# Postnorm decoder layer in fp32: Q and the output projection directly behind V3, the next step's scores ahead of the values

## The chip, the cores and the metric

The kernel runs on one core of a Trainium2 chip. The metric is device time in microseconds of one execution, from inputs in HBM to the output in HBM, as the median of several runs. One execution each was profiled.

## The reference

A decoder layer on x of 4 x 512 x 512 in three parts, each followed by a residual add and a LayerNorm. The change is in the first, a gated slot attention with 16 heads:

```
q, k, v, s, g = x@Wq, x@Wk, x@Wv, clip(x@Ws, -32, 32), x@Wg   # heads of 64, 64, 128, 64, 128
z = cumlogsumexp(s, time); gdec = exp(z[t-1] - z[t]); p = exp(s - z)
hk[t] = hk[t-1]*gdec + k[t] p[t]^T        ; ok[t] = (q[t]/8) hk[t]
pv = softmax(ok)
hv[t] = hv[t-1]*gdec + p[t] v[t]^T        ; o[t] = pv[t] hv[t]
o = o * rsqrt(mean(o^2) + eps) * g_norm_weight * silu(g)
x = layernorm(x + o @ Wo)
```

Then come a cross attention with 32 query heads over ctx_512 and a ternary feed-forward network with 1408 inner units.

## The kernel before

The attention runs as 32 steps n = 0 to 31, each for one pair of heads (n // 4) and one batch element (n % 4) of 512 rows. The recurrences are computed in 8 chunks of 64 rows: products inside a chunk (with a causal mask) plus products with the running state of the chunks before.

Wide products are done as three fp32r matmuls of high and low halves (`mm3`, L61 to L63), in groups of 12 matmuls of 128x512. The projections of step n+1 are woven into step n on TensorE: S, K, V0 to V3 (`VG` to `VG + 3`; values and gate together, one row tile of 128 each) and Q. They alternate between two PSUM banks, so each waits until ScalarE and VectorE have read the group before the last.

Every engine works through its own list in the order of the code; only semaphores hold it. TensorE's list in a step n is: `key_scores` (L1226, products of queries and keys of one chunk), `key_states` (L1243), projections S and K, `slots` (L1295), `states` (L1267), `slots_from_states` (L1307), V0, V1, V2, `transpose_weights` (the slot weights pv, L1153), V3, `diagonals` (L1253), `values_from_states` (L1321), Q, `project_out` (o of the step before times Wo, four row tiles of 6 matmuls), `values` (L1332). `project_out` writes its tiles in turn to two banks, `okb` and `tb`; its tiles 2 and 3 wait until VectorE has added tiles 0 and 1 to acc (`added`). `key_states` of the next step uses the same two banks and waits for all four adds. `key_scores` and `diagonals` both write the two banks `ch`, which VectorE reads with the causal mask (`mask_scores` L1953, `mask_diagonal_blocks` L1971) into the tile `causal`.

The rows of the keys (keys with time on the partitions) are made by VectorE and by DMA: VectorE transposes blocks of 32 (`turn_keys`, into the memory of `causal`), SyncE writes them to HBM (`put_keys`) and reads them back (`get_keys`), and ScalarE copies them (`rows_of_keys`, L1697). The exponentials e, their running sum z and the gated output of the step before go the same way, in the order e, output, z, keys on SyncE's queue. ScalarE's list in the later half of a step is: `high_turned` (high half of the turned output), `rows_of_keys`, the copy and tanh of V3 (L1669, L1671), the copy of Q (L1650), sums of squares. VectorE's is: `low_turned` (L2014), the first half of `inverse_z` (L1939), `mask_diagonal_blocks`, the gating of V3 (L1915), the second half of `inverse_z`, four `add_out` (L2022), `gated_output` (L2076), and then, of the next step, `mask_scores`, the other half of `gated_output`, running key states, clip, `turn_e`, running z and the rest. `mask_diagonal_blocks` also waits for `rows_of_keys`, since the transposed keys lie in `causal`.

The change applies to the steps n <= `LATE_OUT` = 28. From 29 on the order is another, with the output projection ahead of the diagonals.

Of the kernel before, what the change touches and what calls it, by code (L numbers as in the profile page):

```python
# [11 lines left out]
P = 128  # L12
B = 4
# [3 lines left out]
TT = T // P  # L17
# [11 lines left out]
PROJ = 7  # L29
S, K, VG, Q = 0, 1, 2, 6  # L30
# [112 lines left out]
def layer_program(nc, x, ctx_in, Wq, Wk, Wv, Wg, Ws, Wo, gw, gate_w, up_w, down_w, gate_s, up_s, down_s, out,  # L143
# [6 lines left out]
    with ExitStack() as ctx:  # L150
# [10 lines left out]
        def sem(name):  # L161
            return ctx.enter_context(nc.semaphore("a_" + name))
# [14 lines left out]
        keys = sb("keys", [P, T])  # L177
# [3 lines left out]
        eT = sb("eT", [P, 2, T])  # L181
# [11 lines left out]
        running = flat[:, 0:T]  # L193
# [25 lines left out]
        tb = ps[:, 4, :]  # L219
# [36 lines left out]
        proj_done = sem("proj_done")  # L256
        scores_done = sem("scores_done")
        key_states_done = sem("key_states_done")
        keysT_done = sem("keysT_done")
        diag_done = sem("diag_done")  # L260
        states_done = sem("states_done")
        oT_done = sem("oT_done")
# [2 lines left out]
        okT_done = sem("okT_done")  # L265
        pvT_done = sem("pvT_done")
        o_done = sem("o_done")
        e_done = sem("e_done")

        queries_kept = sem("queries_kept")  # L270
        keys_kept = sem("keys_kept")
# [11 lines left out]
        z_turned = sem("z_turned")  # L283
        z_out = sem("z_out")
        z_back = sem("z_back")
        zT_done = sem("zT_done")
        weights_ready = sem("weights_ready")
        eT_ready = sem("eT_ready")
        v_ready = sem("v_ready")
# [783 lines left out]
        def _(pe):  # L1073
# [73 lines left out]
            def max_pair(u, i):  # L1147
                for par in range(2):
                    max_scores(u, u, i, par)

            def transpose4(bank, blocks):
                for i, src in enumerate(blocks):
                    last = pe.transpose(bank[:, i * P:(i + 1) * P], src, ident[:, :])  # L1153
                return last
# [62 lines left out]
            def key_scores(n):  # L1217

                pe.wait_ge(keys_kept, n + 1)
                pe.wait_ge(queries_kept, n + 1)  # L1220
                wait(pe, diag_masked, n)
                for c in range(CHUNKS):
                    i, r = c // 2, c % 2
                    rows = slice(c * CHUNK, (c + 1) * CHUNK)
                    for h in range(2):
                        mm = pe.matmul(ch[h][HALF[r], i * CHUNK:(i + 1) * CHUNK], keys[HALF[h], rows],  # L1226
                                       queries[HALF[h], rows], start=True, stop=True)
                mm.then_inc(scores_done, 1)
# [18 lines left out]
            def diagonals(n):  # L1247

                for c in range(CHUNKS):
                    i, r = c // 2, c % 2  # L1250
                    rows = slice(c * CHUNK, (c + 1) * CHUNK)
                    for h in range(2):
                        mm = pe.matmul(ch[h][HALF[r], i * CHUNK:(i + 1) * CHUNK], eT[HALF[h], n % 2, rows],  # L1253
                                       wT[HALF[h], (c ^ h) * CHUNK:((c ^ h) + 1) * CHUNK], start=True, stop=True)
                mm.then_inc(diag_done, 1)
# [56 lines left out]
            def values_from_states(n):  # L1312

                ob = value_banks(n)
                pe.wait_ge(state_ready, (CHUNKS - 1) * (n + 1))
                if LATE_OUT < n < NSTEP - 1:
                    pe.wait_ge(added, 4 * n)
                for c in range(1, CHUNKS):
                    i, r = c // 2, c % 2
                    for h in range(2):  # L1320
                        pe.matmul(ob[h][HALF[r ^ h], i * P:(i + 1) * P],  # L1321
                                  wT[HALF[h], (c ^ h) * CHUNK:((c ^ h) + 1) * CHUNK],
                                  state[HALF[h], c - 1, :], start=(c == 1 or c == 2), stop=False, skip_group_check=True)

            def values(n, j):

# [9 lines left out]

            def transpose_e(m):
                pe.wait_ge(eT_ready, m + 1)
                transpose4(tb, [eT[:, m % 2, i * P:(i + 1) * P] for i in range(TT)]).then_inc(e_done, 1)

            def transpose_keys(m):
                pe.wait_ge(keys_kept, m + 1)
                wait(pe, wT_ready, m)
                transpose4(okb, [keys[:, i * P:(i + 1) * P] for i in range(TT)]).then_inc(keysT_done, 1)

            def transpose_z():
                pe.wait_ge(scan_done, 1)
                transpose4(ob[0], [running[:, i * P:(i + 1) * P] for i in range(TT)]).then_inc(zT_done, 1)

            def transpose_weights(n):  # L1350
                pe.wait_ge(weights_ready, n + 1)
# [3 lines left out]
            def step(n, p, j, first):  # L1355
                b1, pair1 = (j + 1) % B, p if j < B - 1 else p + 1

                def next_project(*groups):
                    for i in groups:
                        project(n + 1, i, b1, pair1)  # L1360

                into = n == NSTEP - 2
                key_scores(n)
                key_states(n)
                next_project(S, K)
                slots(n)
                states(n, j)
                slots_from_states(n)
                next_project(VG, VG + 1)
                pair0 = p if j else p - 1  # L1370
                if at(n, 0):
                    pe.wait_ge(state_ready, CHUNKS - 1)
                    transpose_x(2, range(KT))
                if at(n, 1):
                    pe.wait_ge(okn_ready, n + 1)
                    transpose_x(3, (0, 1))
                if into:
                    pe.wait_ge(okn_ready, n + 1)
                    transpose_operands(0, 0, 0)
                    transpose_operands(0, 0, 1)  # L1380
                next_project(VG + 2)
                transpose_weights(n)
                if at(n, 1):
                    transpose_x(3, (2, 3))
                if into:
                    pe.wait_ge(opsT_ready, 1)
                    transpose_operands(0, 0, 2)
                    pe.wait_ge(opsT_ready, 2)
                    transpose_operands(0, 0, 3)
                next_project(VG + 3)  # L1390
                if into:
                    pe.wait_ge(opsT_ready, 3)
                    transpose_operands(0, 0, 4)
                    pe.wait_ge(wT_ready, n + 1)
                    max_pair(0, 0)
                if n > LATE_OUT:
                    project_out(n, pair0, (0, 1))
                    if into:
                        max_pair(0, 1)
                    project_out(n, pair0, (2, 3))  # L1400
                pe.wait_ge(wT_ready, n + 1)
                if at(n, 0) or at(n, 1):
                    pe.wait_ge(xlo_ready, (n + 3) * KT)
                if into:
                    pe.wait_ge(opsT_ready, TILES)
                    max_pair(0, 2)
                diagonals(n)
                values_from_states(n)
                if into:
                    max_pair(0, 3)  # L1410
                next_project(Q)
                if not first and n <= LATE_OUT:
                    project_out(n, pair0, (0, 1, 2, 3))
                if into:
                    max_pair(0, 4)
                pe.wait_ge(proj_done, PROJ * (n + 2))
                values(n, j)

            def last_step(n):
# [195 lines left out]
        def _(act):  # L1615
# [34 lines left out]
                nc.scalar.copy(queries[:, :], src).then_inc(queries_kept, 1)  # L1650

            def copy_key_rows(m):
                act.wait_ge(keysT_done, m + 1)
                nc.scalar.copy(key_rows[:, :, :].rearrange("p i c -> p (i c)"), okb)\
                    .then_inc(key_rows_ready, 1)

# [47 lines left out]
                nc.scalar.copy(wT, tb).then_inc(wT_ready, 1)  # L1704

            def copy_e(m):
                act.wait_ge(e_done, m + 1)
                nc.scalar.copy(e[:, :, :].rearrange("p i c -> p (i c)"), tb).then_inc(e_ready, 1)

            def square_sums(n, half):  # L1710
# [156 lines left out]
        def _(dve):  # L1867
# [72 lines left out]

            def first_inverse_z():

                dve.wait_ge(zT_done, 1)
                z = ob[0].rearrange("p (i h m) -> p i h m", i=TT, h=2)
                rows = rz[:, :].rearrange("p (i h m) -> p i h m", i=TT, h=2)
                nc.vector.reciprocal(rows[:, :, 0], z[:, :, 0])
                for r in range(2):
                    nc.vector.reciprocal(rows[HALF[r], :, 1], z[HALF[1 - r], :, 1]).then_inc(rz_ready, 1)
# [69 lines left out]
            def add_out(n, b, tiles):  # L2018
                for t in tiles:
                    wait(dve, wo_done, 4 * (n - 1) + t + 1)  # L2020
                    a = acc[:, TT * b + t, :]
                    nc.vector.tensor_tensor(a, a, out_banks(n)[t % 2], ALU.add).then_inc(added, 1)  # L2022
# [58 lines left out]
            def step(n, p, j, first):  # L2081
# [32 lines left out]
                    low_turned(n)  # L2114
                if late:
                    inverse_z(n + 1, (0,))
                    mask_diagonal_blocks(n)
                gating(n + 1, VG + 3, b1)
                if into:
                    reduce_max(0, 0, 0)  # L2120
# [16 lines left out]
                    norm.apply(dve, j - 1, j - 1, j - 1)  # L2137
                inverse_z(n + 1, (1,) if late else (0, 1))
                if not first and late:
                    add_out(n, (j - 1) % B, (0, 1, 2, 3))  # L2140
                gated_output(n, j, 0)

            def last_step(n):
# [244 lines left out]
```

## Time and profile before

| | us |
|---|---|
| median of 3 runs | 1826.91 (1825.39 to 1828.23) |
| the profiled execution, its time | 1825.38 |
| its span in the trace | 1823.7 |
| TensorE (PE) busy | 1781.5 (98%) |
| VectorE (DVE) busy | 1421.3 (78%) |
| ScalarE (ACT) busy | 754.8 (41%) |
| GpSimd (POOL) busy | 594.2 (33%) |

Busy times are sums over the span; TensorE's matmuls are pipelined, so a record of 0.39 us starts every 0.23 us. A wait is the idle time ahead of an instruction, put down to what released it last. The attention loop takes some 1040 us of the span, the rest is cross attention and feed-forward. PEld is TensorE's loading of weights, SPq SyncE's queue of DMAs. An fp32 matmul of the code stands as two in the records, so 16 matmuls are x32.

### The profile page before, as it was taken

To read this page: it belongs to the slowest core of one execution; us is meant where nothing else is said; L and a number is where in the kernel's file an instruction comes from. 1 tells how busy PE (TensorE), PEld (TensorE's weight loads), DVE (VectorE), ACT (ScalarE), POOL (GpSimd) and SP (SyncE) were. 2 spreads that over 40 slices of the span, in tenths; PEclk is the share of its full clock that TensorE was granted. 3 is DMA by queue.
4 is the path that set the end of the run, shared out by engine and by line. 5 is a ranking of instruction groups with operands and counts; after the bars stand their busy time and mean duration, and the time that the engine had idled before them with its cause. 6 is when DMAs were issued, how large, how long until landed. Compare 5 with 4: busy or idle time off the path is not lost.

```text
span 1823.7 us, 39286 instructions
## 1 busy us (share of the span) xinstructions
PE 1781.5 (98%) x15604; PEld 1303.6 (71%) x15604; DVE 1421.3 (78%) x2555; ACT 754.8 (41%) x1885; POOL 594.2 (33%) x595
## 2 busy tenths in 40 slices
PE   9999999999999999999998799999999999999998
PEld 7788888888887888888886644443434488888886
DVE  5778887878888788888787889999999665555556
ACT  3433333333333333333333248888888622122223
POOL 3042250443332513514432332344423233232332
PEclk9999999999999999999999889999999999999999
DMA  4425334442434252434333001111111111111102
GB/s 149 125 64 145 82 97 113 104 123 77 117 101 126 62 150 77 111 100 120 85 89 96 3 20 29 28 28 29 29 29 20 25 22 29 20 28 25 21 15 92
DMA packets 218550, 127.91 MB, mean 70 GB/s; under 512 B 100096, under 2 KB 198144, under 8 KB 218368
## 3 DMA queue, kind: packets, MB, share of 16 engines
q1 hardware_dynamic: 218368, 125.40, 27.0%
q8 instruction: 124, 2.03, 0.5%
q14 instruction: 58, 0.48, 0.1%
HBM read 72.90 MB, written 44.30 MB: 64 GB/s over the span
## 4 chain that ended last, share of the span: by engine, by line
PE 87%; DVE 5%; ACT 3%; SPq 2%; DMA 2%; issue 1%; POOL 0%; POOLq 0%; DVEq 0%; ACTq 0%
PE a_ps L61 20%; PE a_ps L62 19%; PE a_ps L63 19%; PE a_ps L1137 6%; PE a_ps L1099 5%; PE a_ps L1121 3%; PE a_ps L1081 2%; ACT x_prob L1809 2%; PE a_ps L1332 2%; PE a_ps L1153 2%; PE a_ps L1321 1%; PE a_ps L1267 1%; PE a_ps L1253 1%; PE a_ps L1144 1%; PE a_ps L1295 1%
## 5 line engine op out<-in xcount | busy, mean ns | idle before, releaser
L1873 DVE TENSOR_REDUCE a_raw_qks<-a_ps 128x1 f32<-128x512 f32 x512 | 321.2, 683 | 19.8 <-PE a_ps L1099 19.0
L1809 ACT ACTIVATE x_prob<-a_ps 128x512 f32<-128x512 f32 x512 | 280.0, 609 | 63.4 <-PE a_ps L1121 61.8
L61 PE MATMUL a_ps<-a_vg_hi,a_xT_lo 128*128 128x512 f32 x512 | 207.0, 404 | 0.3 <-DVE a_eT L1910 0.3
L63 PE MATMUL a_ps<-a_vg_hi,a_xT_hi 128*128 128x512 f32 x512 | 200.6, 392 | 0.0
L62 PE MATMUL a_ps<-a_vg_lo,a_xT_hi 128*128 128x512 f32 x512 | 200.1, 391 | 0.0
L917 POOL TENSOR_TENSOR a_f<-a_rs 128x8 f32<-128x8 f32 x32 | 6.4, 199 | 584.6 <-ACT a_flat L1719 584.6
L61 PE MATMUL a_ps<-a_xT_hi,a_qks_lo 128*128 128x512 f32 x384 | 157.2, 409 | 0.4 <-DVE a_xT_lo L1904 0.4
L62 PE MATMUL a_ps<-a_xT_lo,a_qks_hi 128*128 128x512 f32 x384 | 150.7, 392 | 0.0
L63 PE MATMUL a_ps<-a_xT_hi,a_qks_hi 128*128 128x512 f32 x384 | 149.6, 390 | 0.0
L1099 PE MATMUL a_ps<-a_xT_lo,a_xT_hi 64*128 64x512 f32 x384 | 143.8, 462 | 5.1 <-DMA a_xT_lo<-a_xT_lo 2.5
L1719 ACT ACTIVATE a_flat<-a_ps 128x128 bf16<-128x128 f32 x256 | 67.3, 278 | 181.8 <-PE a_ps L1332 174.4
L1121 PE MATMUL a_ps<-a_xT_hi,a_xT_lo 64*128 64x512 f32 x384 | 140.9, 452 | 0.6 <-ACT x_prob L1809 0.5
L2022 DVE TENSOR_TENSOR acc<-acc,a_ps 128x512 f32<-128x512 f32 x128 | 87.2, 683 | 68.9 <-PE a_ps L63 68.5
L61 PE MATMUL a_ps<-a_xT_hi,f_gu_lo 128*128 128x512 f32 x352 | 137.4, 390 | 1.0 <-POOL f_gu_lo L1016 1.0
L1137 PE MATMUL a_ps<-x_prob,x_values 128*32 128x512 f32 x1024 | 137.0, 608 | 0.0
L63 PE MATMUL a_ps<-a_xT_hi,f_gu_hi 128*128 128x512 f32 x352 | 137.0, 389 | 0.0
L62 PE MATMUL a_ps<-f_xT_lo,f_gu_hi 128*128 128x512 f32 x352 | 137.0, 389 | 0.0
L1099 PEld LDWEIGHTS a_ps<-a_xT_lo,a_xT_hi 64*128 64x128 f32 x384 | 61.0, 188 | 101.0 <-issue 42.6
L1669 ACT COPY a_v<-a_ps 128x256 f32<-128x256 f32 x128 | 47.5, 371 | 206.2 <-PE a_ps L63 206.2
L2259 DVE TENSOR_TENSOR acc<-acc,a_ps 128x512 f32<-128x512 f32 x172 | 113.9, 685 | 0.0
L63 PEld LDWEIGHTS a_ps<-a_vg_hi,a_xT_hi 128*128 128x128 f32 x512 | 96.4, 188 | 21.2
L61 PEld LDWEIGHTS a_ps<-a_vg_hi,a_xT_lo 128*128 128x128 f32 x512 | 96.4, 188 | 20.8 <-DVE a_eT L1910 0.4
(205 smaller groups left out, 4107.3 us busy)
## 6 DMA issues: line engine op xcount, KB each, us to landing
a_og_blocks<-a_og_turn SPq DMA_DIRECT2D x120, 128.0 KB, 2.4
a_og_turn<-a_og_blocks SPq DMA_DIRECT2D x30, 512.0 KB, 4.4
a_e_blocks<-a_e_turn SPq DMA_DIRECT2D x124, 64.0 KB, 1.8
a_e_turn<-a_e_blocks SPq DMA_DIRECT2D x31, 256.0 KB, 3.2
a_z_blocks<-a_og SPq DMA_DIRECT2D x124, 64.0 KB, 2.5
a_key_blocks<-a_causal SPq DMA_DIRECT2D x124, 64.0 KB, 3.4
a_causal<-a_key_blocks SPq DMA_DIRECT2D x31, 256.0 KB, 2.8
a_raw_vg<-in_L_attn_Wv_dram SPq DMA_DIRECT2D x8, 512.0 KB, 5.6
```

The lines of the kernel that those rows point to most:

```text
L61: pe.matmul(out, w_lo, x_hi, start=start, stop=False)
L62: pe.matmul(out, w_hi, x_lo, start=False, stop=False)
L63: return pe.matmul(out, w_hi, x_hi, start=False, stop=stop)
L1099: pe.matmul(max_bank(u, q, i, par), qs[q][HALF[par], tile, st * P:(st + 1) * P], ks[q][(tile // 2) ^ par][HALF[par], :], start=True, stop= ...
L1121: pe.matmul(score_bank(q, s, par), ks[q][g ^ par][HALF[par], t * P:(t + 1) * P], qs[q][HALF[par], 2 * g + pair, :], start=True, stop=True) ...
L1137: mm = pe.matmul(avb[32 * i:32 * (i + 1), :], cv[:, q, t, g, :], prob[i % 2][:, (s + i // 2) % 4, :], start=(t == 0), stop=(t == TT - 1))
L1669: nc.scalar.copy(v[:, b % 2, i - VG, :], bank[:, 0:2 * DV]).then_inc(v_ready, 1)
L1719: sq = nc.scalar.activation(squares[:, g, 0:DV], ob[half][:, t * P:(t + 1) * P], ACT.Square, scale=DV ** -0.5, accum_out=crossed_sums[:, t ...
L1809: nc.scalar.activation(prob[par][:, s % 4, :], score_bank(q, s, par), ACT.Exp, scale=X_SCALE).then_inc(exp_done[par], 1)
L1873: nc.vector.tensor_reduce(nm[:, q % 2, i % 4, par, i // 4:i // 4 + 1], max_bank(u, q, i, par), AX.X, ALU.max, negate=True).then_inc(max_re ...
L2022: nc.vector.tensor_tensor(a, a, out_banks(n)[t % 2], ALU.add).then_inc(added, 1)
L2259: nc.vector.tensor_tensor(a, a, down_bank(t), ALU.add).then_inc(f_added, 1)
```

## The change

For n <= 28, TensorE's order behind V3 becomes: Q, `project_out`, `diagonals`, `values_from_states`, `key_scores` of step n+1, `values`, and then `key_states` of step n+1. The wait of `values` for the projections is replaced by one for `values_from_states` (`values_begun`). On VectorE `mask_diagonal_blocks` goes from ahead of V3's gating to between the third and the fourth `add_out`. Three semaphores used once or per prologue are merged into one, `first_turned`.

```diff
@@ values_from_states
-                        pe.matmul(ob[h][HALF[r ^ h], i * P:(i + 1) * P],
+                        mm = pe.matmul(ob[h][HALF[r ^ h], i * P:(i + 1) * P],
...
+                if n <= LATE_OUT:
+                    mm.then_inc(values_begun, 1)
@@ step of TensorE
-                key_scores(n)
+                if first or n > LATE_OUT + 1:
+                    key_scores(n)
                 key_states(n)
...
-                pe.wait_ge(wT_ready, n + 1)
...
+                if n <= LATE_OUT:
+                    next_project(Q)
+                    if not first:
+                        project_out(n, pair0, (0, 1, 2, 3))
+                pe.wait_ge(wT_ready, n + 1)
                 diagonals(n)
                 values_from_states(n)
...
-                next_project(Q)
-                if not first and n <= LATE_OUT:
-                    project_out(n, pair0, (0, 1, 2, 3))
+                if n > LATE_OUT:
+                    next_project(Q)
...
-                pe.wait_ge(proj_done, PROJ * (n + 2))
+                if n <= LATE_OUT:
+                    key_scores(n + 1)
+                    pe.wait_ge(values_begun, n + 1)
+                else:
+                    pe.wait_ge(proj_done, PROJ * (n + 2))
                 values(n, j)
@@ step of VectorE
                 if late:
                     inverse_z(n + 1, (0,))
-                    mask_diagonal_blocks(n)
                 gating(n + 1, VG + 3, b1)
...
                 inverse_z(n + 1, (1,) if late else (0, 1))
                 if not first and late:
-                    add_out(n, (j - 1) % B, (0, 1, 2, 3))
+                    add_out(n, (j - 1) % B, (0, 1, 2))
+                if late:
+                    mask_diagonal_blocks(n)
+                if not first and late:
+                    add_out(n, (j - 1) % B, (3,))
                 gated_output(n, j, 0)
```

TensorE around the end of a step in the middle of the loop, before. `a_flat` holds the slot weights, `a_wo` and `a_oT` are the operands of the output projection; `...` stands for the rest of a group.

```order
L63 MATMUL a_ps<-a_vg_hi,a_xT_hi 128x512
L1253 MATMUL a_ps<-a_flat,a_eT 64x64 [waits a_wT_ready]
L1321 MATMUL a_ps<-a_state,a_flat 64x128 [waits a_state_ready]
L61 MATMUL a_ps<-a_xT_hi,a_qks_lo 128x512 [waits a_q_ready,a_gate_ready]
...
L61 MATMUL a_ps<-a_wo_hi,a_oT_lo 128x512 [waits a_oTlo_ready,a_wo_ready]
...
L61 MATMUL a_ps<-a_wo_hi,a_oT_lo 128x512 [waits a_added]
...
L1332 MATMUL a_ps<-a_v,a_causal 64x128 [waits a_diag_masked,a_proj_done]
L1226 MATMUL a_ps<-a_queries,a_keys 64x64 [waits a_diag_masked,a_queries_kept,a_keys_kept]
L1243 MATMUL a_ps<-a_e,a_key_rows 64x64 [waits a_wT_ready,a_added,a_e_ready,a_key_rows_ready]
```

The same place after the change (its lines are shifted by one or ten).

```order
L63 MATMUL a_ps<-a_vg_hi,a_xT_hi 128x512
L61 MATMUL a_ps<-a_xT_hi,a_qks_lo 128x512 [waits a_q_ready,a_gate_ready]
...
L61 MATMUL a_ps<-a_wo_hi,a_oT_lo 128x512 [waits a_oTlo_ready,a_wo_ready]
...
L61 MATMUL a_ps<-a_wo_hi,a_oT_lo 128x512 [waits a_added]
...
L1252 MATMUL a_ps<-a_flat,a_eT 64x64 [waits a_wT_ready]
L1320 MATMUL a_ps<-a_state,a_flat 64x128 [waits a_state_ready]
L1225 MATMUL a_ps<-a_queries,a_keys 64x64 [waits a_diag_masked,a_queries_kept,a_keys_kept]
L1333 MATMUL a_ps<-a_v,a_causal 64x128 [waits a_diag_masked,a_values_begun]
L1242 MATMUL a_ps<-a_e,a_key_rows 64x64 [waits a_wT_ready,a_added,a_e_ready,a_key_rows_ready]
```

Diagonals and values from states moved behind the output projection, and the scores of the next step ahead of the values.

VectorE in the same part of the step, before: low half of the turned output, `inverse_z`, mask, V3's gating, `inverse_z`, the adds, the gated output.

```order
L2014 TENSOR_TENSOR a_oT_lo<-a_og_turn,a_oT_hi 128x4x8x32 [waits a_oThi_ready]
L1939 RECIPROCAL a_rz<-a_og 128x2x4x32 [waits a_weights_ready,a_z_back]
L1971 TENSOR_TENSOR a_causal<-a_ps,a_mask 128x256 [waits a_key_rows_ready,a_diag_done]
L1971 TENSOR_TENSOR a_causal<-a_ps,a_mask 128x256
L1915 SCALAR_TENSOR_TENSOR a_gate<-a_gate,a_ps 128x256 [waits a_tanh_ready]
L1939 RECIPROCAL a_rz<-a_og 128x2x4x32
L2022 TENSOR_TENSOR acc<-acc,a_ps 128x512 [waits a_wo_done] x4
L2076 TENSOR_TENSOR a_og<-a_ps,a_gate 128x4x128 [waits a_rz_ready,a_o_done]
```

And after:

```order
L2023 TENSOR_TENSOR a_oT_lo<-a_og_turn,a_oT_hi 128x4x8x32 [waits a_oThi_ready]
L1948 RECIPROCAL a_rz<-a_og 128x2x4x32 [waits a_weights_ready,a_z_back]
L1924 SCALAR_TENSOR_TENSOR a_gate<-a_gate,a_ps 128x256 [waits a_tanh_ready]
L1948 RECIPROCAL a_rz<-a_og 128x2x4x32
L2031 TENSOR_TENSOR acc<-acc,a_ps 128x512 [waits a_wo_done] x3
L1980 TENSOR_TENSOR a_causal<-a_ps,a_mask 128x256 [waits a_key_rows_ready,a_diag_done]
L1980 TENSOR_TENSOR a_causal<-a_ps,a_mask 128x256
L2031 TENSOR_TENSOR acc<-acc,a_ps 128x512 [waits a_wo_done]
L2085 TENSOR_TENSOR a_og<-a_ps,a_gate 128x4x128 [waits a_rz_ready,a_o_done]
```

The mask moved behind three of the four adds.

## Rows read from the trace of the kernel before

**Rows 1.** Stretches: length, busy us of each engine, granted clock, DMA share, GB/s.
```profile
99.07:940.43 841.36, 840.76 (x9505) 689.35 (x9505) 683.44 (x1242) 280.08 (x918) 284.24 (x236) 1.00 0.39 103
49.60:56.40 6.80, 5.50 (x21) 5.11 (x22) 4.34 (x11) 2.86 (x5) 0.00 (x0) 0.50 0.69 193
```

**Rows 2.** TensorE's timeline of one step: start, duration, line, operands, count.
```profile
503.87 1.10 PE L1332 MATMUL a_ps<-a_v,a_causal 64*64 64x128 f32 x32
504.80 0.64 PE L1226 MATMUL a_ps<-a_queries,a_keys 64*64 64x64 f32 x32
505.26 0.65 PE L1243 MATMUL a_ps<-a_e,a_key_rows 64*64 64x64 f32 x28
...
524.74 0.39 PE L63 MATMUL a_ps<-a_vg_hi,a_xT_hi 128*128 128x512 f32 x1
525.06 0.69 PE L1253 MATMUL a_ps<-a_flat,a_eT 64*64 64x64 f32 x32
525.57 1.05 PE L1321 MATMUL a_ps<-a_state,a_flat 64*64 64x128 f32 x28
526.55 0.50 PE L61 MATMUL a_ps<-a_xT_hi,a_qks_lo 128*128 128x512 f32 x1
...
532.17 0.39 PE L61 MATMUL a_ps<-a_wo_hi,a_oT_lo 128*128 128x512 f32 x1
...
534.98 1.10 PE L1332 MATMUL a_ps<-a_v,a_causal 64*64 64x128 f32 x32
```

**Rows 3.** ScalarE's timeline of the same step: key rows, and V3's tanh.
```profile
527.75 0.62 ACT L1697 COPY a_key_rows<-a_causal 128x512 f32<-128x512 f32 x1 [2.57 <-DMA a_causal<-a_key_blocks]
...
528.54 0.39 ACT L1671 ACTIVATE a_gate<-a_ps 128x256 f32<-128x256 f32 x1
```

**Rows 4.** VectorE's timeline of the same step.
```profile
525.22 1.23 DVE L2014 TENSOR_TENSOR a_oT_lo<-a_og_turn,a_oT_hi 128x1024 fp32r<-128x1024 f32 x1 [1.82 <-ACT a_oT_hi L1685]
...
528.48 0.76 DVE L1971 TENSOR_TENSOR a_causal<-a_ps,a_mask 128x256 f32<-128x256 f32 x2 [0.37 <-ACT a_key_rows L1697]
529.15 0.41 DVE L1915 SCALAR_TENSOR_TENSOR a_gate<-a_gate,a_ps 128x256 f32<-128x256 f32 x1
529.48 1.75 DVE L1939 RECIPROCAL a_rz<-a_og 128x256 f32<-128x256 f32 x1
531.14 0.63 DVE L2022 TENSOR_TENSOR acc<-acc,a_ps 128x512 f32<-128x512 f32 x1
```

**Rows 5.** Waits in the 27 steps: us in total, times, longest.
```profile
ACT a_key_rows L1697 <- DMA a_causal<-a_key_blocks: 72.3, 27, 3.9
```

**Rows 6.** The chain that ended last, in the slowest of the 27 steps.
```profile
535.97 0.15 PE a_ps L1332 x4
...
552.34 4.88 DMA a_key_blocks<-a_causal
...
559.97 0.63 ACT a_key_rows L1697
...
563.43 0.56 DVE acc L2022
...
564.03 0.50 PE a_ps L61
```

**Rows 7.** Timelines: `values` ahead of, and key rows in, the first and last step.
```profile
99.07 1.10 PE L1332 MATMUL a_ps<-a_v,a_causal 64*64 64x128 f32 x32
...
122.79 0.62 ACT L1697 COPY a_key_rows<-a_causal 128x512 f32<-128x512 f32 x1 [2.95 <-DMA a_causal<-a_key_blocks]
...
909.32 1.10 PE L1332 MATMUL a_ps<-a_v,a_causal 64*64 64x128 f32 x32
...
932.67 0.62 ACT L1697 COPY a_key_rows<-a_causal 128x512 f32<-128x512 f32 x1 [2.40 <-DMA a_causal<-a_key_blocks]
```

**Rows 8.** The same two timelines of the step with the least distance.
```profile
878.22 1.10 PE L1332 MATMUL a_ps<-a_v,a_causal 64*64 64x128 f32 x32
...
901.14 0.62 ACT L1697 COPY a_key_rows<-a_causal 128x512 f32<-128x512 f32 x1 [2.33 <-DMA a_causal<-a_key_blocks]
```

More of the change, by code:

```diff
@@ L258, in layer_program @@
         key_states_done = sem("key_states_done")
-        keysT_done = sem("keysT_done")
         diag_done = sem("diag_done")
@@ L267, in layer_program @@
         o_done = sem("o_done")
-        e_done = sem("e_done")
+        first_turned = sem("first_turned")
         queries_kept = sem("queries_kept")
@@ L285, in layer_program @@
         z_back = sem("z_back")
-        zT_done = sem("zT_done")
+        values_begun = sem("values_begun")
         weights_ready = sem("weights_ready")
@@ L1338, in transpose_e @@
                 pe.wait_ge(eT_ready, m + 1)
-                transpose4(tb, [eT[:, m % 2, i * P:(i + 1) * P] for i in range(TT)]).then_inc(e_done, 1)
+                transpose4(tb, [eT[:, m % 2, i * P:(i + 1) * P] for i in range(TT)]).then_inc(first_turned, 1)
             def transpose_keys(m):
@@ L1343, in transpose_keys @@
                 wait(pe, wT_ready, m)
-                transpose4(okb, [keys[:, i * P:(i + 1) * P] for i in range(TT)]).then_inc(keysT_done, 1)
+                transpose4(okb, [keys[:, i * P:(i + 1) * P] for i in range(TT)]).then_inc(first_turned, 1)
             def transpose_z():
                 pe.wait_ge(scan_done, 1)
-                transpose4(ob[0], [running[:, i * P:(i + 1) * P] for i in range(TT)]).then_inc(zT_done, 1)
+                transpose4(ob[0], [running[:, i * P:(i + 1) * P] for i in range(TT)]).then_inc(first_turned, 1)
             def transpose_weights(n):
@@ L1652, in copy_key_rows @@
             def copy_key_rows(m):
-                act.wait_ge(keysT_done, m + 1)
+                act.wait_ge(first_turned, 2)
                 nc.scalar.copy(key_rows[:, :, :].rearrange("p i c -> p (i c)"), okb)\
@@ L1706, in copy_e @@
             def copy_e(m):
-                act.wait_ge(e_done, m + 1)
+                act.wait_ge(first_turned, 1)
                 nc.scalar.copy(e[:, :, :].rearrange("p i c -> p (i c)"), tb).then_inc(e_ready, 1)
@@ L1941, in first_inverse_z @@
             def first_inverse_z():
-                dve.wait_ge(zT_done, 1)
+                dve.wait_ge(first_turned, 3)
                 z = ob[0].rearrange("p (i h m) -> p i h m", i=TT, h=2)
```

## Prediction

> **What bounds the kernel now.** I read the waits first, then TensorE's timeline of one step, then ScalarE's and VectorE's of the same step. The change touches the 29 steps n = 0 to 28 of the attention loop. Of these, 27 (n = 2 to 28) look alike: they fill 841.36 us, 31.16 us each, with TensorE busy for 840.76 of them at a granted clock of 1.00 [rows 1]. So TensorE has almost no idle time, and what could be won on it is only the cost of changing between 128x128 and 64x64 work. The second thing to see is how near a loop over the other engines comes. I count it from the end of `values` of the step before, which I call zero. In the step of rows 2 it is 503.87 + 1.10 = 504.97. From there VectorE works through gating, masks, running sums and transposes, SyncE sends the keys through HBM, and ScalarE copies the key rows at 527.75, that is K = 22.78 after zero [rows 2, 3]. Only behind that copy, in ScalarE's order, stand V3's copy and tanh, so V3's gating on VectorE comes at 529.15, the second half of `inverse_z` at 529.48, and the first `add_out` at 531.14, ending 531.77 [rows 4]. TensorE needs that add to reuse its bank for the third tile of the output projection, which starts at 532.17 [rows 2]. **The slack of this loop is 0.35 us of 31.** ScalarE waited for the keys' transfer in all 27 steps, 72.3 us in all [rows 5]. In the slowest step the slack is used up: the chain runs from `values` over the write of the keys (4.88 us) to the key rows at 559.97, the add at 563.43 (to 563.99) and TensorE's third tile at 564.03 [rows 6].
>
> How firmly is K tied to zero? In [rows 7] the first and the last of the 27 steps have K = 122.79 - 100.17 = 22.62 and 932.67 - 910.42 = 22.25; the least is 901.14 - 879.32 = 21.82 [rows 8], the largest 559.97 - 536.12 = 23.85 [rows 6]. The mean over all 27, read one by one in this way, is 22.5.
>
> **The change, part by part.**
>
> *One stretch of 64x64 work less.* Diagonals and values from states stood alone between V3 and Q; now they, the next scores, `values` and the key states are one stretch. Entering costs 525.06 - 524.74 = 0.32 against the usual pitch of 0.23, so 0.09. Leaving: the 28 records of L1321 take 526.55 - 525.57 = 0.98; at the 0.029 a record that L1332 shows (504.80 - 503.87 over 32) they would take 0.81, so 0.17, and the first wide matmul behind lasts 0.50 and not 0.39, so 0.11 more [rows 2]. Together 0.37 us a step gained on TensorE, as long as nothing waits.
>
> *A wait inside the new stretch.* `key_scores` of the next step writes the banks that `mask_diagonal_blocks` reads. Before, Q and the four output tiles (some 8 us) stood between and hid the mask at no cost. Now only values from states do. From the first diagonal: its group drains after 0.69, a semaphore takes 0.05 (from the add's end 563.99 to 564.03), the two masks 0.76, the semaphore back 0.05 [rows 4, 6]: 1.55. TensorE's own work up to there is 0.51 + 0.81 = 1.32. So 0.23 us of waiting, on the path. The lower bound is 0; the upper is 0.9, if VectorE is still in an add of 0.63 when the diagonals are done. I take 0.23: the third add begins with its tile's end, 1.9 us before the diagonals drain.
>
> *Q and the output projection earlier.* Q (12 matmuls, 2.72) starts right behind V3. V3 ends at 524.74 + 0.23, 20.0 after zero, and now 19.5, since the scores (0.46) no longer stand at the step's start. V2's gating, which frees Q's bank, lies on VectorE before an idle stretch of 1.82 that ended at 525.22 [rows 4], so 18.4 after zero: no wait. The low half of the turned output ended at 525.22 + 1.23, 21.5 after zero; the output projection now starts at 22.3: no wait either. The third tile could then start at 22.3 + 2.72 = 25.0. But it still needs the first add.
>
> *The first add does not move with them.* Nothing between `values` and the key rows is moved but one thing: the keys' transfer starts from VectorE's transposes, whose chain begins at zero. Behind the key rows, VectorE's mask leaves the way: tanh ends at 528.54 + 0.39 = 528.93 against a gating at 529.15 [rows 3, 4], so gating comes 0.18 earlier. The add then ends K + 1.22 (gating) + 0.33 + 1.66 + 0.63 = K + 3.84, and TensorE's third tile starts at **K + 3.89**. With K = 22.5 that is 26.4, **1.4 us after TensorE could**. This stall is new, once in every step.
>
> *What follows the third tile.* Before: two tiles and the entry, 534.98 - 532.17 = 2.81, then `values` [rows 2]. Now: 2.81, plus 0.11 since the first matmul after a pause is the long kind (0.50) [rows 6]; 1.55 for diagonals, values from states and the wait for the mask; 0.46 for the scores (505.26 - 504.80); and `values` itself 1.10: 6.03. So the loop of one step is K + 3.89 + 6.03 = **K + 9.92 = 32.42 us**, against 31.16. What was moved from beside the loop (scores, diagonals) now stands in it, behind the add.
>
> *Small things.* Key states need the fourth add: it ends 0.6 after the scores start, before they are asked for. The semaphores merged into one and the wait for `values_begun` cost nothing: that work is 0.46 us old by then. POOL's weight splits at each fourth step are released by V3 or Q and have the same room. SyncE's order is untouched. Step 1 is longer by its x transposes, so TensorE bounds it: -0.2. Steps 0 and 29 together: -0.2. The phases behind the attention are unchanged.
>
> **Sum**: 27 x (32.42 - 31.16) = +34.0, -0.4: +33.6 us. On the profiled execution 1825.4 + 33.6 = 1859.0; it stood 1.5 under the median of the runs, so on the median **1860.5**.
>
> **Rivals.**
>
> *A. TensorE stays the bound* (faster). Then a step is V3's end at 19.5, + 5.44 (Q and two tiles) + 5.92 (the 6.03 above without the restart) = 30.9, and 27 x -0.26 - 0.4 = -7: 1820. For it speaks that TensorE is busy 840.76 of 841.36. It needs K under 21.1, since K + 3.89 must be at most 25.0; the least of 27 was 21.8. The Trainium skill (TensorEngine Tiling (Array Packing), Key Properties) says that changing the tiling mode drains TensorE, by which dropping one of the stretches is a gain in every step; the trace agrees with the drain, and by that rule alone the time would be A's. The skill's price of a DMA (DMA: Bandwidth & Descriptors, about 2.0 us fixed and 436 GB/s) would make the keys' 256 KB a write of 2.6 us; that would give A's time too, but the row of the slowest step says 4.88.
>
> *B. The loop starts earlier than I count* (slower, but less). The projections now begin 0.46 us earlier after `values`, since the scores are already done. If K is really held by them (keys copied by ScalarE behind the K projection) it falls by up to 0.46: 27 x 0.46 = 12.4 less, 1848. Against it: the chain of the slowest step runs through VectorE from `values`, not through TensorE. A mix with shorter transfers could bring it near no change at all.
>
> *C. The loop is longer* (slower by more). Two pauses a step shift the transfers against each other, and the keys land as in the slowest step, K 1.35 later. In half of the steps: +18, 1879.
>
> *D. The clock falls.* In the beginning the granted clock was 0.50 (1.2 GHz) for 6.8 us behind steps with idle time [rows 1]: about 3.4 us lost each time. Once a step would be +92, 1950. The pauses here are short and TensorE stays busy over 95%, so I hardly believe it.
>
> **Chances.** Forecast 0.55 (1852 to 1868, by K between 22.2 and 22.8); A 0.12; B 0.17, of which 0.04 near no change; C 0.13; D 0.03. A run tells apart about 0.2%, 3.7 us. Faster 0.12, same 0.04, slower 0.84. The range leaves out A, D and the outer end of C: 1837 to 1880.
>
> **What the profile after would show.** Right: TensorE's L61 of the output projection waits for the add on VectorE in some 27 steps, 1.2 to 1.5 us each, and L1225 (key scores) for the mask, about 0.2; K stays at 22.5 after `values`; the period is near 32.4; the mask no longer waits for the key rows. Wrong: no wait of TensorE for the add (A), K near 22.0 (B), K above 23 (C), a clock of 0.50 in these steps (D).

## The result and the profile after

| | before | changed |
|---|---|---|
| median of 4 runs each, us | 1826.41 | 1865.82 (1864.95 to 1866.26) |
| ratio to before, 95% interval | | 1.0209 (1.0196 to 1.0221) |
| span of the profiled execution, us | 1823.7 | 1864.5 |
| the 27 steps n = 2 to 28, us | 841.36, 31.16 each | 880.78, 32.62 each |
| K, from the end of `values` to the key rows, mean of 27 | 22.48 | 22.53 |

The changed kernel is slower by 39.4 us; the forecast was 33.6. The spans of the two profiled executions differ by 40.8, and of these 880.78 - 841.36 = 39.4 lie in the 27 like steps.

The stretch of these steps after the change, to be laid beside [rows 1] (length, busy us of PE, PEld, DVE, ACT and POOL, granted clock, DMA share, GB/s). TensorE is busy for 849.41 of 880.78, so it has 31 us of idle time, where it had 0.6.

```profile
99.93:980.71 880.78, 849.41 (x9518) 687.88 (x9512) 679.19 (x1242) 278.40 (x918) 285.81 (x236) 1.00 0.37 99
```

The waits of the changed kernel in the same stretch (us in total, times, longest). L2031 is `add_out`, L1980 the mask of the diagonals, L1252 the diagonals, L1706 the key rows, L1924 the gating.

```profile
ACT a_key_rows L1706 <- DMA a_causal<-a_key_blocks: 72.5, 27, 3.8
...
PEld a_ps L61 <- DVE acc L2031: 39.2, 27, 2.5
...
DVE a_causal L1980 <- PE a_ps L1252: 36.1, 27, 1.4
...
PE a_ps L61 <- DVE acc L2031: 27.8, 27, 2.1
...
DVE a_gate L1924 <- ACT a_gate L1680: 23.0, 26, 1.7
...
PEld a_ps L61 <- DVE a_gate L1924: 10.8, 27, 0.6
```

ScalarE waits for the keys as long as before, 72.5 us against 72.3 [rows 5]. What is new is below it: in each of the 27 steps TensorE waits for the first add, and in 26 of them VectorE waits for V3's tanh, which stands behind the key rows. One step of the changed kernel, first TensorE (start, duration), to be laid beside [rows 2]:

```profile
523.92 1.08 PE L1333 MATMUL a_ps<-a_v,a_causal 64*64 64x128 f32 x32
...
551.53 0.50 PE L61 MATMUL a_ps<-a_wo_hi,a_oT_lo 128*128 128x512 f32 x1 [1.19 <-DVE acc L2031]
...
554.52 0.69 PE L1252 MATMUL a_ps<-a_flat,a_eT 64*64 64x64 f32 x32
555.03 1.05 PE L1320 MATMUL a_ps<-a_state,a_flat 64*64 64x128 f32 x28
556.18 0.69 PE L1225 MATMUL a_ps<-a_queries,a_keys 64*64 64x64 f32 x32
556.67 1.08 PE L1333 MATMUL a_ps<-a_v,a_causal 64*64 64x128 f32 x32
```

and then ScalarE and VectorE, which answer to [rows 3, 4]:

```profile
547.63 0.62 ACT L1706 COPY a_key_rows<-a_causal 128x512 f32<-128x512 f32 x1 [2.57 <-DMA a_causal<-a_key_blocks]
...
548.42 0.39 ACT L1680 ACTIVATE a_gate<-a_ps 128x256 f32<-128x256 f32 x1
```

```profile
548.85 0.42 DVE L1924 SCALAR_TENSOR_TENSOR a_gate<-a_gate,a_ps 128x256 f32<-128x256 f32 x1 [0.86 <-ACT a_gate L1680]
549.18 1.75 DVE L1948 RECIPROCAL a_rz<-a_og 128x256 f32<-128x256 f32 x1
550.85 1.22 DVE L2031 TENSOR_TENSOR acc<-acc,a_ps 128x512 f32<-128x512 f32 x2
...
555.28 0.76 DVE L1980 TENSOR_TENSOR a_causal<-a_ps,a_mask 128x256 f32<-128x256 f32 x2 [1.35 <-PE a_ps L1252]
```

`values` of the step before ends at 525.00. The key rows follow 22.63 later, and from there the rows are a straight line: tanh, gating, `inverse_z`, add, and TensorE at 551.53. That the two first adds stand as one piece of 1.22 shows that both tiles had long been ready. The chain that ended last says the same for the whole program. Its shares by engine, from the page of the kernel before:

```profile
PE 87%; DVE 5%; ACT 3%; SPq 2%; DMA 2%; issue 1%; POOL 0%; POOLq 0%; DVEq 0%; ACTq 0%
```

And from the page of the changed kernel, by engine and by line:

```profile
PE 48%; DVE 20%; SPq 12%; DMA 10%; ACT 5%; issue 4%; POOL 0%; DVEq 0%; POOLq 0%; ACTq 0%
PE a_ps L61 9%; SPq L623 8%; PE a_ps L63 8%; PE a_ps L62 8%; PE a_ps L1136 5%; PE a_ps L1098 5%; DMA a_key_blocks<-a_causal 5%; DMA a_causal<-a_key_blocks 4%; DVE a_og L2085 3%; DVE a_flat L1932 3%; DVE a_rz L1948 3%; PE a_ps L1120 3%; DVE a_key_state L1971 2%; PE a_ps L1080 2%; SPq L756 2%
```

Now 42% of the chain is VectorE, SyncE's queue and DMAs, and of the DMAs' 10% the keys have 9. The loop that had 0.35 us of slack is the bound.

### The profile page after: what moved, and what is told of

Same layout as the page of the kernel before. It is cut to its first block, busy times and chain, and to the rows that moved or that the text cites. A ratio compares the mean times of both kernels' runs of the same rounds, so it can differ in the third digit from the quotient of the medians.

```text
span 1864.5 us, 39284 instructions
## 1 busy us (share of the span) xinstructions
PE 1791.6 (96%) x15604; PEld 1303.4 (70%) x15604; DVE 1417.4 (76%) x2555; ACT 753.1 (40%) x1885; POOL 596.9 (32%) x595
## 4 chain that ended last, share of the span: by engine, by line
PE 48%; DVE 20%; SPq 12%; DMA 10%; ACT 5%; issue 4%; POOL 0%; DVEq 0%; POOLq 0%; ACTq 0%
PE a_ps L61 9%; SPq L623 8%; PE a_ps L63 8%; PE a_ps L62 8%; PE a_ps L1136 5%; PE a_ps L1098 5%; DMA a_key_blocks<-a_causal 5%; DMA a_causal<-a_key_blocks 4%; DVE a_og L2085 3%; DVE a_flat L1932 3%; DVE a_rz L1948 3%; PE a_ps L1120 3%; DVE a_key_state L1971 2%; PE a_ps L1080 2%; SPq L756 2%
## 5 line engine op out<-in xcount | busy, mean ns | idle before, releaser
L61 PE MATMUL a_ps<-a_xT_hi,a_qks_lo 128*128 128x512 f32 x384 | 153.3, 399 | 0.4 <-DVE a_xT_lo L1913 0.4
L61 PE MATMUL a_ps<-a_wo_hi,a_oT_lo 128*128 128x512 f32 x256 | 104.7, 409 | 30.3 <-DVE acc L2031 28.7
L2031 DVE TENSOR_TENSOR acc<-acc,a_ps 128x512 f32<-128x512 f32 x128 | 83.3, 670 | 40.9 <-PE a_ps L63 40.6
L2271 DVE TENSOR_TENSOR acc<-acc,a_ps 128x512 f32<-128x512 f32 x172 | 113.8, 685 | 0.0
```

What stands on the lines that cost most here:

```text
L61: pe.matmul(out, w_lo, x_hi, start=start, stop=False)
L2271: nc.vector.tensor_tensor(a, a, down_bank(t), ALU.add).then_inc(f_added, 1)
```

## Experiments

The theory: a loop runs from the end of `values` over VectorE, the keys' transfers, V3's tanh, `inverse_z` and the first add back to TensorE, and the change put diagonals, mask and scores into it behind the add. The rivals: the long stretch of small matmuls with the wait for the mask inside is itself the cost; or the key rows don't hold V3's gating. All kernels compute the whole layer. The kernel before ran beside each group: 1828.0 (beside x_order_only to x_inv_v3), 1827.5 (beside the last four rows of the table). Steps are those of the one profiled execution of each kernel. The edits below are shown as they act in the steps up to 28: the conditions that keep the other steps as they were are left out, and `...` stands for lines between.

| kernel | median, us | ratio to before (95%) | us a step, 27 steps |
|---|---|---|---|
| before | 1828.0 / 1827.5 | | 31.16 |
| changed | 1865.8 | 1.0209 (1.0196 to 1.0221) | 32.62 |
| x_order_only | 1851.0 | 1.0122 (1.0108 to 1.0136) | 32.10 |
| x_scores_only | 1837.7 | 1.0051 (1.0039 to 1.0064) | 31.49 |
| x_inv_late | 1832.8 | 1.0029 (1.0018 to 1.0040) | 31.36 |
| x_inv_v3 | 1830.7 | 1.0014 (1.0005 to 1.0023) | 31.26 |
| x_v3_first | 1837.0 | 1.0052 (1.0039 to 1.0065) | 31.56 |
| x_gate | 1824.1 | 0.9981 (0.9973 to 0.9990) | 31.03 |
| x_states | 1819.3 | 0.9957 (0.9944 to 0.9970) | 30.93 |
| x_before_inv | 1825.0 | 0.9983 (0.9974 to 0.9992) | 31.12 |

**One part undone: the scores back behind the values.**

```diff
-                if first or n > LATE_OUT + 1:
-                    key_scores(n)
+                key_scores(n)
...
-                    key_scores(n + 1)
                     pe.wait_ge(values_begun, n + 1)
```

> The changed kernel with one part undone: the next step's scores stand again behind the values (at the head of the step), Q and the output projection stay directly behind V3. Theory (loop over the key rows and the first add): the loop is shorter by the scores alone, 0.46 us in 27 steps, so 1865.8 - 12.4 = 1853; TensorE still waits about 1.1 to 1.3 us a step for the first add. Rival (the long stretch of small matmuls with the wait for the mask inside it is what costs): most of the 39 us goes away, under 1840.

Measured 1851.0, 14.9 less than the changed kernel, and 0.52 us a step where 0.46 was expected. In its profile TensorE waits for the first add in 24 steps, 21.2 us in all, about 0.9 each, less than the 1.1 to 1.3 that I had written. So of the 39 us some 15 are the scores inside the loop. The rest stays without them, and the rival that wanted the time under 1840 falls.

**One part alone: the scores ahead of the values in the kernel before.**

```diff
-                key_scores(n)
                 key_states(n)
...
                 next_project(Q)
                 project_out(n, pair0, (0, 1, 2, 3))
...
+                key_scores(n + 1)
-                pe.wait_ge(proj_done, PROJ * (n + 2))
+                pe.wait_ge(values_begun, n + 1)
                 values(n, j)
```

The kernel also has the new wait of `values` and the merged semaphores of the change.

> The kernel before with one part of the change: only the next step's scores are moved ahead of the values; diagonals, values from states and the mask stay where they were. Theory: the scores now lie in the loop behind the first add, whose slack was 0.35 us against their 0.46; steps whose key rows come later than 22.5 us after the values lose some tenths, the others nothing: 1826 to 1833. Rival (scores between the output projection and the values save nothing and cost nothing): 1826 within 2.

Measured 1837.7, 5 us above the range. The mean step is 31.49, 0.33 longer. TensorE waits for the first add in only 7 steps, as the theory says, but there is a second wait, in all 27 steps, that I hadn't expected:

```profile
PEld a_ps L61 <- DVE a_gate L1921: 10.9, 27, 0.6
PEld a_ps L61 <- DVE acc L2028: 3.7, 7, 0.9
```

It is V2's projection, which needs its bank from V0's gating. Since the scores no longer stand at the head of the step, the projections begin 0.46 us earlier, but V0's gating comes as late after `values` as before. So this is a second loop with little slack. The 0.46 us are paid behind the adds, and of the 0.46 gained at the head of the step the pause ahead of V2 takes more than half: V3 starts 16.95 after `values`, against 17.15 before (means of 27).

**One operation taken out of the loop on VectorE.**

```diff
-                inverse_z(n + 1, (1,))
-                add_out(n, (j - 1) % B, (0, 1, 2))
+                add_out(n, (j - 1) % B, (0, 1))
+                inverse_z(n + 1, (1,))
+                add_out(n, (j - 1) % B, (2,))
                 mask_diagonal_blocks(n)
                 add_out(n, (j - 1) % B, (3,))
```

> The changed kernel with one operation of VectorE moved: the second half of inverse_z goes from ahead of the first output add to behind the second one. Theory: the first add comes 1.66 us earlier, TensorE's wait for it is gone in most steps, a step takes the larger of 31.0 and K + 8.4 with K near 22.5, so 31.0 to 31.3 and 1822 to 1830. Rival (long stretch of small matmuls or the mask wait is the cost): still over 1855.

Measured 1832.8: one operation of 1.75 us, moved behind two others on an engine that isn't the busiest, gives back 33 of the 39 us. TensorE's wait for the add falls from 27 steps to 5 (the row of PEld). It is 3 us above the range, and the V2 wait is here too. The rival (over 1855) falls: the long stretch of small matmuls is the same in this kernel, and so is the wait for the mask inside it, with the scores starting 1.15 after values from states, in the mean of 27 steps, in both kernels.

```profile
PEld a_ps L61 <- DVE a_gate L1924: 10.8, 27, 0.6
PEld a_ps L61 <- DVE acc L2031: 2.5, 5, 0.8
```

**V3 ahead of the key rows on ScalarE as well, and alone.**

```diff
-                rows_of_keys(n + 1)
-                next_proj(VG + 3)
+                next_proj(VG + 3)
+                rows_of_keys(n + 1)
```

With the late `inverse_z`:

> The same as x_inv_late, and ScalarE copies V3 and takes its tanh ahead of the key rows, not behind them. Theory: the key rows are out of the loop, all 27 steps take TensorE's own time of 30.9 to 31.0 us, 1820 to 1823, a little faster than the kernel before. If something else than the key rows held V3's gating (VectorE's own list), it is no faster than x_inv_late.

Alone, on the changed kernel:

> The changed kernel with one thing moved on ScalarE: V3's copy and tanh ahead of the key rows. VectorE's order stays as changed, with both halves of inverse_z ahead of the first add. Theory: the key rows are out of the loop, and VectorE's own list now sets the first add: low half of the output (ends 21.2 us after the values on average), then 1.66 + 0.33 + 1.66 + 0.63 for inverse_z, gating, inverse_z and the add, so 25.5, and with the 6.25 us measured from the add to the end of the values 31.7 a step: 1840 to 1846. If the key rows weren't the link that holds V3's gating, it stays at 1865.

Alone it gives 1837.0, 29 us less than the changed kernel and 3 us below the range: 31.56 a step, with the low half of the output ending 21.0 after `values`. So V3's place behind the key rows is the link; nothing else was moved. Together they give 1830.7, 31.26 a step: no wait for the add is left, but the time is 8 us above the range and the 30.9 aren't reached. It is 2.1 us under x_inv_late, with intervals that overlap, so the gain of this move on top of the late `inverse_z` shows in the profile (five waits less) and hardly in the time. What is left shows in TensorE's timeline of one step of x_inv_v3: V2 begins with a long first matmul, 0.31 and not 0.23 behind the one before it,

```profile
518.65 0.39 PE L63 MATMUL a_ps<-a_vg_hi,a_xT_hi 128*128 128x512 f32 x1
518.96 0.50 PE L61 MATMUL a_ps<-a_vg_hi,a_xT_lo 128*128 128x512 f32 x1
519.30 0.39 PE L62 MATMUL a_ps<-a_vg_lo,a_xT_hi 128*128 128x512 f32 x1
```

and 519.30 - 518.96 = 0.34 to the next, again not 0.23: 0.08 of waiting, and 0.11 that I call the restart. In the mean of 27 steps it is 0.12 and 0.11, so 0.2 us a step for a wait that hardly shows as idle time. In the kernel before and in x_order_only, where the scores stand at the head of the step, both distances are 0.23. The other part is the wait for the mask ahead of the scores:

```profile
533.80 1.05 PE L1320 MATMUL a_ps<-a_state,a_flat 64*64 64x128 f32 x28
534.95 0.69 PE L1225 MATMUL a_ps<-a_queries,a_keys 64*64 64x64 f32 x32
```

534.95 - 533.80 = 1.15 for work of 0.81: 0.34.

**The V2 wait taken away.** On x_inv_v3, VectorE gates V0 one operation earlier:

```diff
+                gating(n + 1, VG, b1)
                 turn_keys(n + 1)
-                gating(n + 1, VG, b1)
```

> x_inv_v3 with V0's gating on VectorE ahead of the transposes of the keys. x_inv_v3 took 31.26 us a step; its V2 projection started with a long first matmul behind V0's gating in all 27 steps, about 0.1 of waiting and 0.11 of restart. Theory: both go, 31.05 a step, 5 to 6 us less than x_inv_v3, 1825. Rival (the pause is taken up by the wait for the mask or another one later): within 1 us of x_inv_v3.

Measured 1824.1, 31.03 a step: 6.6 us less, where 5 to 6 were expected. The wait is gone from the list, and both distances at V2 are 0.23. This version is faster than the kernel before by 0.19%, interval 0.10 to 0.27%.

**The wait for the mask taken away.** On x_gate, the key states of the next step go between values from states and the scores, and the fourth add goes ahead of the mask, since the key states need its bank:

```diff
                 values_from_states(n)
...
+                key_states(n + 1)
                 key_scores(n + 1)
...
                 values(n, j)
```
```diff
-                add_out(n, (j - 1) % B, (2,))
-                mask_diagonal_blocks(n)
-                add_out(n, (j - 1) % B, (3,))
+                add_out(n, (j - 1) % B, (2, 3))
+                mask_diagonal_blocks(n)
```

> x_gate with the key states of the next step moved too, in between values from states and the scores, and the fourth output add on VectorE ahead of the mask. Theory: the 0.4 us of key states hide the mask, so TensorE's wait ahead of the scores (0.34 us a step in the changed kernel) is gone: 30.75 a step, 1816 to 1819, faster than the kernel before by 0.4 to 0.6%. Rival: the start of the projections another 0.4 us earlier is lost again at V2 or at the output projection, which waits for the turned output: 1824 or more.

Measured 1819.3, 0.3 above the range and the fastest kernel here, 0.43% (0.30 to 0.56) faster than before. Its timeline of one step shows the scores starting while the last key states still run:

```profile
530.74 0.84 PE L1320 MATMUL a_ps<-a_state,a_flat 64*64 64x128 f32 x24
...
531.53 0.61 PE L1242 MATMUL a_ps<-a_e,a_key_rows 64*64 64x64 f32 x22
531.93 0.26 PE L1225 MATMUL a_ps<-a_queries,a_keys 64*64 64x64 f32 x2
```

The step is 30.93, not the 30.75 expected. The rival has its share: V2 waits again, since the projections begin another 0.4 us earlier.

```profile
PEld a_ps L61 <- DVE a_gate L1929: 7.4, 27, 0.5
```

Its other half, the wait for the turned output, came in one step, for 1.0 us.

**The kernel before with more slack.**

```diff
-                inverse_z(n + 1, (1,))
-                add_out(n, (j - 1) % B, (0, 1, 2, 3))
+                add_out(n, (j - 1) % B, (0, 1))
+                inverse_z(n + 1, (1,))
+                add_out(n, (j - 1) % B, (2, 3))
```

> The kernel before with the second half of inverse_z behind the second output add. Theory: its loop gets 1.66 us more slack, so that the steps with late key rows (31.37 and 32.00 us in the profile) shrink to 31.11: 1 to 2 us faster at most, not to be told from no change. If the kernel before was held by VectorE more than the profile shows, it gains more than 4 us.

Measured 1825.0, 2.5 us less (0.17%, 0.08 to 0.26%), 31.12 a step against 31.16. The profile accounts for about 1 us of it. More than 4 us, the sign that VectorE held the kernel before more than its profile shows, didn't come. So the kernel before was where [rows 6] put it, just at the edge, with a loss only in single steps: PEld waits for an add in 3 of its 27 steps, and in none of x_before_inv.

## Why the prediction held, and where it was off

**What bounds the kernel.** Right. A loop with 0.35 us of slack was read from [rows 2, 4], and everything that the change puts behind the add went into the step. x_inv_late and x_v3_first each cut one link and each give back most of the loss.

**K is tied to the end of `values`.** Right, and this decided against rival B: the projections did begin 0.46 us earlier, yet K went from 22.48 to 22.53. K was 22.4 to 22.5 in all the experiments, with steps from 30.93 to 32.62 us. But a link in the middle was left out. The prediction has the keys' transfer start from VectorE's transposes. In the changed kernel those of the keys end 13.4 after `values` in the mean, and SyncE begins to issue the keys' writes only at 14.8. Ahead of them in its list stand the writes of the turned output and of z and the reads of e and the output, and it issues these without a pause from the moment the output is turned. In the step shown that is 534.85, 9.85 after `values`, and its rows are:

```profile
534.88 2.40 SPq L623 DMA_DIRECT2D a_og_blocks<-a_og_turn  x4
537.32 0.45 SPq L628 DMA_DIRECT2D a_e_turn<-a_e_blocks  x1
537.87 1.87 SPq L623 DMA_DIRECT2D a_z_blocks<-a_og  x4
539.78 0.43 SPq L628 DMA_DIRECT2D a_og_turn<-a_og_blocks  x1
540.31 1.92 SPq L623 DMA_DIRECT2D a_key_blocks<-a_causal  x4
```

x_gate bears this out: its transposes of the keys end 0.3 later, at 13.7, and the issue stays at 14.8 and K at 22.4. So what ties K to `values` is VectorE's chain up to the turned output, and then SyncE's list. No run has a shorter list, or the keys ahead of z in it.

**The first add at K + 3.84.** Measured K + 3.84 in the mean of 27 steps.

**TensorE's stall of 1.4 us.** The idle rows give 27.8 / 27 = 1.03; a record of a wide matmul reaches 0.16 beyond its pitch, so 1.19. The difference is V2's wait, which the prediction didn't have and which made TensorE come 0.2 us later. It cost nothing here, since TensorE waits for the add anyway.

**The terms behind the add** were 0.16 us short together, 27 x 0.16 = 4.3 of the 5.8 us by which the forecast was short:

| from, to | predicted | measured, mean of 27 |
|---|---|---|
| end of the first add to the first diagonal | 0.05 + 2.92 = 2.97 | 3.01 |
| first diagonal to mask | 0.69 + 0.05 = 0.74 | 0.76 |
| mask to the end of `values` | 0.76 + 0.05 + 0.46 + 1.10 = 2.37 | 2.47 |

The largest is the step of the mask's wait. I took one semaphore, 0.05, from the mask's end to TensorE. In the step shown the mask ends at 556.04 and the scores start at 556.18, 0.14 later, and `values` starts 0.49 behind them, not 0.46. So a stretch of small matmuls pays for a restart too, about 0.1 us; I had counted one only for the wide matmuls. K came 0.03 later than the 22.5 of the sum, which is another 0.8 us.

**The gain of one stretch less (0.37 us)** can't be seen in the changed kernel, where it vanishes in the wait for the add. In x_states, where both waits are away but some of V2's is left, the step is 0.23 us shorter than before. That is consistent with 0.37 less some 0.15 for V2, but it isn't a measurement of the 0.37.

**Rival A (1820)** would have been wrong in its number, had its case come. x_inv_v3 is that case, with TensorE no longer held by the add, and it takes 31.26 a step and 1830.7 us, slower than the kernel before. So dropping one stretch did not by itself give the time of A. The sum for A left out V2's bank (0.2 us a step) and had the mask's wait at 0.23 where 0.34 was measured. I had asked for each wait that now comes earlier behind V3, but not for the projections at the head of the step, which come earlier too. Nor would a write of 2.6 us for the keys have given A's time, as the prediction says: in the slowest step it takes 4.88 - 2.6 = 2.3 off, and 23.85 - 2.3 = 21.6 is still over the 21.1 that A needs.

**The other steps.** Predicted -0.4 together; up to the end of step 1 the changed kernel gained 0.2, step 29 took 0.5 less. Steps 30 and 31 took 1.9 us more in this profile (68.2 against 66.3), at a mean granted clock of 0.87 against 0.92 in that stretch. All the other kernels were longer there than the kernel before too, 66.7 to 69.1, at 0.85 to 0.90, and x_before_inv, whose order in these steps is that of the kernel before, took 67.5. One profile of each doesn't show whether the change has a part in this; the cause stays open. **Rivals C and D** didn't happen: K stayed, and the granted clock was 1.00 in the 27 steps.

## What to carry to other kernels

An engine that is busy 99.9% of a stretch can still be a third of a microsecond from being held by a loop over all the others; before you move work on it, follow the loop through the slowest step and see on which side of the loop's last wait the moved work lands. Here work put ahead of the wait was hidden, and work put behind it was paid in full.

If a reordering loses, look at what stands ahead of the late link on the other engines' lists before undoing it: here four short moves on ScalarE and VectorE and one on TensorE turned 2.1% slower into 0.4% faster. And when a stretch starts earlier, check every buffer that it waits for.

## What the hardware showed that I had not expected

A wait on TensorE costs more than its idle row says. The first matmul behind one lasts 0.50 and not 0.39, even where the pause itself was 0.08 us (V2 in x_inv_v3). So that wait cost 0.2 us a step, 6.6 us in the time between x_inv_v3 and x_gate, and among the waits of x_inv_v3 it stands in no row of PE, only in this one of PEld:

```profile
PEld a_ps L61 <- DVE a_gate L1927: 10.4, 27, 0.6
```

A stretch of 64x64 matmuls that stood ready behind a wait started 0.14 us after what it waited for, against 0.05 for the wide ones.
